# Relative values of an attention layer: from eight shifts across the whole array to four column tiles, with the shift picked by a DMA

## What is computed

```
rel_pos = arange(L)[None, :] - arange(L)[:, None] + 255
rel_k, rel_v = relative_k[rel_pos], relative_v[rel_pos]     # L x L x 16, tables of 511 rows
scores = einsum('bhld,bhrd->bhlr', Q, K) * scale + einsum('bhld,lrd->bhlr', Q, rel_k)
attn = softmax(scores)
out = einsum('bhlr,bhrd->bhld', attn, V) + einsum('bhlr,lrd->bhld', attn, rel_v)
```

## Time and profile before

| | |
|---|---|
| median of the runs | 3597.58 us |
| the profiled execution itself | 3588.57 us |
| its span in the trace | 3586.8 us |
| `project`, up to the first step of `attend` | about 230 us |
| `attend`, 512 units | about 2790 us |
| `mix` | about 566 us |
| TensorE matmul busy | 3292.6 us, 92% of the span |
| VectorE, ScalarE, GpSimd busy | 2736.0, 2629.0, 2195.9 us |

### The profile page before, as it was taken

How to read it: one execution, slowest core, us unless ns; L and a number is a source line. 1 busy time by engine, 2 the same in 40 slices (tenths; PEclk the granted TensorE clock), 3 DMA queues, 4 the chain that set the end, 5 groups by cost and what they waited for, 6 DMA issues and landing times. The chain is left out here.

```text
span 3586.8 us, 166713 instructions
## 1 busy us (share of the span) xinstructions
PE 3292.6 (92%) x65430; PEld 2603.2 (73%) x65430; DVE 2736.0 (76%) x7853; ACT 2629.0 (73%) x5852; POOL 2195.9 (61%) x2407
## 2 busy tenths in 40 slices
PE   7599999999999999999999999999999996999990
PEld 4367777777777777777777777777777775579980
DVE  6488888888888888888888888888888886534443
ACT  3288888888888888888888888888888884334440
POOL 0167777777777777777777777777777764810006
PEclk9779999999999999999999999999999998579995
DMA  6766666666666666666666666666666664722124
GB/s 211 231 215 212 211 211 214 215 210 208 212 212 214 213 214 212 210 211 211 212 210 209 212 211 210 212 212 215 212 209 211 215 208 142 270 71 65 61 63 143
DMA packets 356377, 701.33 MB, mean 196 GB/s; under 512 B 59545, under 2 KB 168706, under 8 KB 355346
## 3 DMA queue, kind: packets, MB, share of 16 engines
q1 hardware_dynamic: 349458, 673.92, 58.1%
q0 software_dynamic: 6144, 16.79, 1.4%
HBM read 343.02 MB, written 347.46 MB: 193 GB/s over the span
## 5 line engine op out<-in xcount | busy, mean ns | idle before, releaser
L851 POOL TENSOR_TENSOR pt_near<-pt_full,pt_near 128x512 f16<-128x512 f32 (+3 forms) x1984 | 1839.4, 956 | 780.2 <-DVE pt_near L1156 779.5
L1063 ACT ACTIVATE pt_full<-pb,exp_bias 128x512 f32<-128x512 f32 x2048 | 1316.1, 694 | 437.3 <-PE pb L946 395.0
L1136 DVE TENSOR_REDUCE part_max<-pb 128x1 f32<-128x512 f32 (+3 forms) x1376 | 770.0, 573 | 155.4 <-PE pb L904 153.7
L999 PE MATMUL pb<-pt_near,table_high 128*128 128x64 f16 (+6 forms) x18432 | 833.7, 187 | 0.9 <-DVE rel_out L1189 0.8
L1132 DVE CUSTOM_DVE_ANT_0 near_sum<-pb,skewed 128x512 bf16<-128x512 f32 (+3 forms) x1216 | 675.2, 571 | 200.6 <-PE pb L904 175.4
L999 PE MATMUL pb<-pt_near,table_low 128*128 128x64 f16 (+6 forms) x9216 | 818.2, 187 | 0.0
L999 PEld LDWEIGHTS pb<-pt_near,table_high 128*128 128x128 f16 x18432 | 790.5, 97 | 1.1 <-DVE rel_out L1189 0.9
L999 PEld LDWEIGHTS pb<-pt_near,table_low 128*128 128x128 f16 x9216 | 772.7, 97 | 0.0
L938 PE MATMUL pb<-ident,skewed 128*128 128x128 f32 x3840 | 648.4, 287 | 48.9 <-ACT pt_full L1063 39.1
L972 PEld LDWEIGHTS pb<-v_head,pt_near 128*128 128x128 f16 x13440 | 432.2, 96 | 188.0 <-POOL pt_near L851 97.4
L972 PE MATMUL pb<-v_head,pt_near 128*128 128x33 f16 x13440 | 514.7, 178 | 13.9 <-POOL pt_near L851 7.0
(11 more groups left out here) (183 smaller groups left out, 4102.0 us busy)
## 6 DMA issues: line engine op xcount, KB each, us to landing
skewed<-rel_scratch SPq DMA_DIRECT2D x256, 576.0 KB, 5.5
rel_scratch<-rel SPq DMA_DIRECT2D x416, 319.5 KB, 3.4
rel_scratch<-rel SPq DMA_DIRECT2D x320, 320.0 KB, 2.8
skewed<-rel_scratch SPq DMA_DIRECT2D x64, 512.0 KB, 4.7
skewed<-rel_scratch SPq DMA_DIRECT2D x64, 448.0 KB, 4.3
k_stack<-planes_scratch SPq DMA_DIRECT2D x192, 96.0 KB, 4.9
planes_scratch<-planes SPq DMA_DIRECT2D x64, 256.0 KB, 2.3
rel_scratch<-rel SPq DMA_DIRECT2D x64, 256.0 KB, 2.7
```

The source lines that it names most:

```text
L851: ins = nc.gpsimd.tensor_tensor(pt_piece(c, 1, a, z, near), pt_full[e][:, (a - 4 * g) * P:(z - 4 * g) * P], pt_piece(c, 0, a, z, near), AL ...
L999: ins = nc.tensor.matmul(acc[:, c0:c1, :], keep[table][:, w:w + P], pt_near[half][:, part, c0:c1, d - M_LO, a * SHIFTS:(a + 1) * SHIFTS], ...
L1063: nc.scalar.activation(pt_full[e][:, :], x_ps[e % 2][:, :], ACT.Exp, bias=exp_bias[:, 0:1]).then_inc(s_exp, 1)
L1136: ins = nc.vector.tensor_reduce(best, src, axis=AX.X, op=ALU.max)
```

## The change

- The pass over the relative values is turned round. The probabilities become the stationary operand: up to 8 blocks times 4 queries that lie 32 apart, at most 32 columns, so an instruction uses one of four column tiles of the array (output partitions 32t to 32t+31). The table is the moving operand: 4 shifts 32 rows apart times 16 dimensions, 64 columns. Query offset q0 = 4j + t goes to column tile t in step j.
- A half then takes 8 steps x 9 distances x 3 products x 4 tiles = 864 matmuls, and 3 more where a window is cut in two: 867 instead of 432, 108 a step instead of 54.
- The mask and the f32 pick matmuls are gone. VectorE copies the whole bank once a half (`rel_values_out`), SyncE stores it to HBM (256 KB) and, a step later, reads the wanted shift back with four DMAs whose access pattern takes the right 16 numbers of each row (`picked_src`). GpSimd adds and scales (`output`), three steps after the store.
- `rel_values` moves from the end of the step to between the relative products (that is, after pair 0 of the turned scores, T) and the first values, except in the first of its eight steps.
- `pt_near` is laid out by distance, then block, so that the stationary operand is a strided run; the blocks of the first half are stored in reverse (`row_of`), which also changes the order of the rows that `mix` reads. The number of elements converted or subtracted by the other engines stays.

The core of the diff:

```
-SHIFTS = P // DK
-SHIFT_GROUPS = P // SHIFTS
+SHIFTS = 4
+SHIFT_STEP = P // SHIFTS
+COL_TILES = 4
+COL_TILE = P // COL_TILES
+RV_ROW = SHIFTS * P + DK
...
-LAG_SEL = LAG_RV + HALF_C
-LAG_O = LAG_SEL + 1
+LAG_SEL = LAG_RV + HALF_C + 1
+LAG_O = LAG_SEL + 3
...
-        pt_near = [sb(f"pt_near{i}", [P, 2, HALF_C, REL_BLOCKS, P], FP16) for i in range(2)]
+        pt_near = [sb(f"pt_near{i}", [P, 2, REL_BLOCKS, HALF_C, P], FP16) for i in range(2)]
...
+                h, i = half_at(k, LAG_SEL)
+                if i == 0 and h >= 0 and exists(it, h * HALF_C):
+                    sp.wait_ge(s_rle, h + 1)
...
+                    sp.dma_start(hbm["rel_values"][h % 2, :, 0:CH], rel_raw[h % 2][:, :]).then_inc(s_rw[h % 2], 16)
+                if i == 1 and h >= 0 and exists(it, h * HALF_C):
+                    sp.wait_ge(s_rw[h % 2], 16 * (h // 2 + 1))
...
+                    for tile in range(COL_TILES):
+                        sp.dma_start(rel_sum[h % 2][tile:P:COL_TILES, :, :],
+                                     picked_src(h % 2, tile)).then_inc(s_rr[h % 2], 16)
...
-                for d in order:
-                    c0, c1 = half_range(half, d)
-                    w = table_window(d, a) * DK
-                    for n, (table, part) in enumerate((("table_high", 0), ("table_high", 1), ("table_low", 0))):
-                        ins = nc.tensor.matmul(
-                            acc[:, c0:c1, :], keep[table][:, w:w + P],
-                            pt_near[half][:, part, c0:c1, d - M_LO, a * SHIFTS:(a + 1) * SHIFTS],
...
+                for d in (0, 1, -1, -2, 2, -3, -4, -5, -6):
+                    n_rows = half_rows(half, d)
+                    for n, (name, part) in enumerate((("table_high", 0), ("table_high", 1), ("table_low", 0))):
+                        table = keep[name][:, :].rearrange("p (n d) -> p n d", d=DK)
+                        probs = pt_near[half][:, part, d - M_LO, :, :].rearrange("p c l -> p (c l)")
+                        for tile in range(COL_TILES):
+                            q0 = COL_TILES * j + tile
+                            acc = r_ps[tile * COL_TILE:tile * COL_TILE + n_rows * SHIFTS,
+                                       j * SHIFTS * DK:(j + 1) * SHIFTS * DK].rearrange("p (s d) -> p s d", s=SHIFTS)
+                            for a, z, col in table_windows(d, q0):
+                                ins = nc.tensor.matmul(
+                                    acc[:, a:z, :], probs[:, q0:n_rows * P:SHIFT_STEP],
+                                    table[:, col:col + (z - a - 1) * SHIFT_STEP + 1:SHIFT_STEP, :],
+                                    start=(j == 0 and d == 0 and n == 0), stop=(j == HALF_C - 1 and d == M_LO and n == 2))
...
+                    if pair == 0 and rel_on and j:
+                        rel_values(it, h, j)
...
-                if rel_on:
-                    for quarter in range(4):
-                        rel_values(it, h, j, quarter)
-                h, j = half_at(k, LAG_SEL)
-                if h >= 0 and j == 0 and exists(it, h * HALF_C):
-                    for i in range(HALF_C):
-                        pick_values(it, h, i)
+                if rel_on and j == 0:
+                    rel_values(it, h, j)
...
-            def mask_values(it, h, part):
...
+            def rel_values_out(it, h):
+
+                dve.wait_ge(s_rl, h + 1)
                 if h >= 2:
...
+                    dve.wait_ge(s_rw[h % 2], 16 * (h // 2))
+                nc.vector.tensor_copy(rel_raw[h % 2][:, :], r_ps[:, :]).then_inc(s_rle, 1)
```

More of the change, by code:

```diff
@@ L112, in table_window, with table_windows @@
     return LEFT_N + j - MAIN0
+def table_windows(d, q0):
+    cols = [table_column(d, q0 + SHIFT_STEP * (SHIFTS - 1 - s)) for s in range(SHIFTS)]
+    cut = next((s for s in range(1, SHIFTS) if cols[s] != cols[s - 1] + SHIFT_STEP), SHIFTS)
+    return [(a, z, cols[a]) for a, z in ((0, cut), (cut, SHIFTS)) if a < z]
 LAG_S, LAG_A, LAG_X, LAG_PV = 3, 4, 5, 6
 LAG_RV = LAG_PV + HALF_C - 1
-LAG_SEL = LAG_RV + HALF_C
-LAG_O = LAG_SEL + 1
+LAG_SEL = LAG_RV + HALF_C + 1
+LAG_O = LAG_SEL + 3
 PEEL = LAG_O + 1
@@ L168, in pieces, with row_of, half_rows @@
     return out
-def half_range(half, d):
-    cs = [c for c in range(half * HALF_C, (half + 1) * HALF_C) if 0 <= c + d < NB]
-    return cs[0] - half * HALF_C, cs[-1] + 1 - half * HALF_C
+def row_of(c):
+    return HALF_C - 1 - c if c < HALF_C else c - HALF_C
+def half_rows(half, d):
+    rows = sorted(row_of(c) for c in range(half * HALF_C, (half + 1) * HALF_C) if 0 <= c + d < NB)
+    assert rows == list(range(len(rows)))
+    return len(rows)
 def segments(c):
@@ L360, in _ @@
         def _(pool):
-            ident, pick, shift_mask = keep["ident"], keep["pick"], keep["shift_mask"]
+            ident = keep["ident"]
             nc.gpsimd.memset(keep["blank"][:, :], 0.0).then_inc(s_id, 1)
@@ L364, in _ @@
             nc.gpsimd.memset(ident[:, :], 0.0).then_inc(s_pre, 1)
-            nc.gpsimd.memset(pick[:, :], 0.0).then_inc(s_pre, 1)
-            nc.gpsimd.memset(shift_mask[:, :], 1.0).then_inc(s_pre, 1)
-            pool.wait_ge(s_pre, 3)
+            pool.wait_ge(s_pre, 1)
             nc.gpsimd.affine_select(out=ident[:, :], in_=ident[:, :], compare_op=ALU.not_equal,
                                     fill=1.0, base=0, pattern=[[-1, P]], channel_multiplier=1).then_inc(s_id, 1)
[L370 to L381, removed]
         @block.scalar
@@ L620, in attend @@
         s_rle = sem("b_rel_values_on_chip")
-        s_sel = sem("b_rel_values_picked")
+        s_rw = [sem(f"b_rel_values_stored{i}") for i in range(2)]
+        s_rr = [sem(f"b_rel_values_picked{i}") for i in range(2)]
         s_o1 = sem("b_out_steps")
@@ L1006, in pick_values @@
[L1006 to L1018 removed]
+                if j == 0:
+                    if h:
+                        pe.wait_ge(s_rle, h)
+                    u = h * HALF_C + HALF_C - 1
+                    wait_low(pe, it, u, E - 2)
+                    wait_low(pe, it, u, E - 1)
```

135 lines of the change are left out of this document (54 added, 81 removed).

## The result

The changed kernel takes 4296.05 us, the median of 4 runs (4281.47 to 4307.22), beside 3597.78 us before. The ratio is 1.193 (1.190 to 1.197). The forecast was 3420 us, faster; the measured time also lies above the upper end of the range, 3900. The profiled execution took 4294.29 us, with a span of 4293.0.

A forecast was written before the change was run, and what follows sets the result against it. TensorE's own order was taken to bound the kernel at 5.51 us a unit with waits; afterwards a TensorE-ScalarE loop of 5.16 us would, saving 0.35 us a unit, 179 us over 512 units: 3420 us, range 3330 to 3900.

The forecast's parts named there:

- The loop: Attention unit: pair 0, relative values, pair 1 of turned scores on TensorE, then ScalarE's exponentials and `q_max`; 5.16 us a unit.
- The sum: Attention unit: 2.83 us for pair 0 to pair 1's end, plus ScalarE, relative values, passage and waits, less transposes: 5.16 us.
- The terms of ScalarE: In the attention unit: 0.03 us to the first exponential, 1.45 for exponentials and `q_max`, 0.05 back to TensorE.
- The passage to another way of dividing the array: TensorE, between relative values and the whole-array values behind them: costs 0.10 us, added in seven steps of eight.
- Four in a row stream side by side at 29 ns a group: Relative values on TensorE: four column tiles run at once, so 27 groups at 29 ns make a step of 0.78 us.
- their weight loads are hidden: TensorE: 97 ns weight loads hide behind 64-column matmuls starting 28 to 29 ns apart.
- my break-even of 42 ns: Relative values: if a group of four column tiles takes over 42 ns, the change loses.
- two at a time: Rival, relative values: only two column tiles run at once, 1.57 us a step, 3823 us; chance 0.14, including 42 to 65 ns.
- What isn't shown is eight instructions in every 29 ns: Relative values on TensorE: caveat that no row shows this instruction rate over a whole step; the sum still takes 0.78 us.
- The clock row drops: Sign in the changed profile: a lower clock row in the attention stage would show the prediction wrong; no size given.
- DMAs: Store (2.7 us) and pick (4.8 us) of relative values are covered, with no GpSimd wait for a DMA.
- four tiles one after the other: Rival, relative values: column tiles run in turn, 2.78 us a step instead of 0.78, 4443 us; chance 0.16.

## Why the prediction was wrong

**The loop: right.** In the unit of the timeline, pair 0 to the end of pair 1 without the relative values is 4.33 - 1.76 = 2.57 us. The sum has 2.83 for nine transposes; this unit has seven, which takes off 0.16 to 0.20, and 0.06 to 0.10 more is gone that I can't place. The terms of ScalarE came out within 0.02 us (1.43 for 1.45, 0.03 and 0.05 as taken). The new place alone gave 3738.5 us beside 3745 expected, and ScalarE and TensorE wait where I said they would; the wait of the values for GpSimd fell from 85.0 to 17.1 us. The passage to another way of dividing the array is there as well: the last group starts at 1527.83 and the values 0.18 us later, 0.12 more than a group's 0.06, where I took 0.10.

**"Four in a row stream side by side at 29 ns a group": the first step that failed.** They do run side by side, but I took "their weight loads are hidden" from whole-array loads of contiguous columns. Here the columns lie 64 bytes apart, and the load sets the pitch: 63 ns for 32 columns, 57 for a group of two, 33 for 16, and 30 when the 32 lie side by side. By my break-even of 42 ns, which no run tested by itself, the group is too long. The rival "two at a time" had nearly this pitch (2 x 29 = 58 ns) for a reason that the experiments exclude. The rule of the Trainium skill that I weighed there (TensorE: Matmul & The Clock Gate, Part 3, "What overlaps and what doesn't": a weight load overlaps running matmuls only when its row group differs) isn't what happens either: four contiguous loads into the same row groups cost 30 ns together with their matmuls, though each load is recorded with 105 ns, so they are hidden.

This alone explains a small part. From the one unit, 5.84 - 5.51 = 0.33 us, 169 us over 512 units, the estimate is 3767 us; with the 5.58 us of the mean undisturbed unit it is 3634. The range held either. And with the pitch at 30 ns the time was 4313 all the same.

**"What isn't shown is eight instructions in every 29 ns": the second, and the larger one.** I named it as a bound on the pitch of a group, and put it at nothing in the sum. It shows as stalls of up to 3.8 us, 0.76 us of 6.93 a unit: most stand in the burst of relative values itself (168 of 273 us), the others behind it. (1) The stalls stand before lines that wait for no engine. (2) Three edits that change what the array does leave the time within 1.5% (4296, 4327, 4313, 4359 us), and the stalls grow as the groups get shorter. (3) With fewer instructions in a step they are nearly gone (9 us with two tiles), and spreading a burst takes 5% off. (4) Every stall over 0.9 us ends at the border of a block of 256 instructions, shortly after a packet of the instruction queue has landed, in kernels with column tiles and in one without. So the stalls are TensorE waiting for its instructions; that is shown.

It isn't the mean rate that decides. The changed kernel gets through 62400 / 2500 = 25.0 matmuls a microsecond with 273 us of stalls; the kernel before with its matmuls cut in two makes 24.8 with 52, and 26.8 go through spread out (66933) with 228. What goes with the stalls is how many blocks of 256 instructions run in under 3.4 us: 8 of 487 in the kernel with 52 us of stalls, 44 of 527 in the one with 228, and 175 of 490 in the changed one. The page has the queue: 732 packets of 11.99 MB, 16 KB each, where the kernel before has `q8 instruction: 522, 8.55, 1.1%`. The Trainium skill (Runtime: NRT & Kernel Launch, "Instruction fetch mechanics") describes such fetching in blocks of 16 KiB, and the packet size agrees; it calls the cost mostly hidden, which held before the change and doesn't hold here.

What stays open is why a packet comes as late as it does. Spread out, half of the blocks ahead of a stall ran for 3.9 us or more, longer than the 3.4 us between packets at their closest, so something else delays a packet too. Whether the kernel's other DMA traffic does, I didn't try.

**"The clock row drops": foreseen as a sign, not priced.** It has a price of its own. TensorE spends 645 of the 2500 us at the level of 0.50, and units with some of it and no stall last 6.86 us beside 5.58. The stalls bring most of it about: kernels with under 10 us of stalls have 0.99 to 1.00. But they don't set it alone. With half the moving columns the stalls were 261 us and the clock 0.81, with all of them 273 and 0.87. Of the 6.93 us, 5.58 are the undisturbed unit and 0.76 stalls; the 0.59 left are the lower clock, other waits and units with more transposes, which I didn't separate.

**The rest.** Place: with the step as long as it is, the end of the step would have been better by 94 us. DMAs: no wait of GpSimd for the picked values is in the list, as forecast. The chance of 0.33 for slower was given to the right side for partly wrong reasons, and no rival joined a longer group with stalls. That the rival "four tiles one after the other" comes near the measured time (4443 us) is luck: it wants some 103 ns a group, and a group takes 63.

## What to carry to other kernels

A halved amount of work on the array in twice as many instructions isn't a halved cost. Price a burst of short matmuls by its weight loads (columns, and the stride they are read at), and by how fast it runs through 256 instructions of TensorE, that is 128 matmuls with their loads. In the kernel before no block of 256 ran in under 5.1 us and none stalled; in the changed kernel a third ran in under 3.4 us. In a profile look for "issue" idle time that no engine explains. Before work is moved into a loop between two engines, add up the loop: a quarter of the work in the new place gained 3%, all of it lost 4%.

## What the runs showed of the hardware that was not expected

- Weight loads into column tiles of 128 x 32 f16 cost 63 ns for a group of four when the columns lie 64 bytes apart, 30 ns when they lie side by side. With 24 columns and the stride it is 50 ns (1527.14 - 1526.99 = 0.15 us for three groups), so about 1.6 ns a column, for four tiles at once.
- That pitch doesn't go by the clock: at a granted clock of 0.50 three groups still start within 1520.71 - 1520.52 = 0.19 us, while the four transposes took 1.11 us instead of 0.66.
- Whole-array matmuls don't start closer than 25 ns, with 33 moving columns or with 32 down to 8; groups of four column tiles start 30 ns apart, so 7.5 ns a matmul with its load.
- TensorE gets its instructions in packets of 256. One that isn't there in time stops it for up to 4.3 us, even between a weight load and its matmul; it goes on some 0.9 to 1.8 us after the packet has landed. Packets didn't start closer than 3.2 us in any of these kernels. Behind the stall of 1.92 us the granted clock was 0.50.
